# Attention and bitlinear FFN on eight cores: one clamp folded away and the transposed activations evicted by ScalarE alone

## What is computed

```python
def _act_quant(x):
    scale = 127.0 / jnp.clip(jnp.max(jnp.abs(x), axis=-1, keepdims=True), 1e-05)
    xq = jnp.clip(jnp.round(x * scale), -128.0, 127.0) / scale
    return x + jax.lax.stop_gradient(xq - x)

def _bitlinear(x, w):
    return jnp.einsum('bsi,oi->bso', _act_quant(x), _weight_quant(w))

gate = silu(_bitlinear(x, w_gate))          # 1024 -> 4096
up = _bitlinear(x, w_up)                    # 1024 -> 4096
ffn = _bitlinear(gate * up, w_down)         # 4096 -> 1024
x = _layernorm(x + ffn)
```

## Time and profile before

| | |
|---|---|
| median of 3 runs | 3895.15 us |
| profiled execution, its own time | 3897.07 us |
| span of its slowest core (core 3) | 3895.5 us |
| spans of the other cores | 3872.5 to 3888.9 us |
| core 3: TensorE busy | 1803.9 us (46%) |
| core 3: VectorE busy | 1509.8 us (39%) |
| core 3: ScalarE busy | 978.6 us (25%) |
| core 3: mean granted TensorE clock | 0.664 of full |

### The profile page before, as it was taken

One profiled execution on the slowest core, in us unless ns is written; L12 is line 12 of the kernel. 1 busy time (PEld: TensorE's weight loads), 2 busy tenths in 40 slices (PEclk: granted clock), 3 DMA queues, 4 the chain that ended last, 5 costly groups with the idle time before them and its releaser, 6 DMA issues.

```text
span 3895.5 us, 32053 instructions; the slowest of 8 cores (3872.5 to 3895.5 us)
## 1 busy us (share of the span) xinstructions
PE 1803.9 (46%) x8824; PEld 608.9 (16%) x8824; DVE 1509.8 (39%) x2965; ACT 978.6 (25%) x1164; POOL 18.7 (0%) x54
## 2 busy tenths in 40 slices
PE   1201212321034434565776775484466529552944
PEld 0000000100011111111111111232133204221421
DVE  1453474444455544322122112444244344424443
ACT  1202201220000014574875785110011001101100
POOL 1000000000000000000000000000000000000000
PEclk9998555555565555555555555697788769785967
DMA  5445343322410000101001000321242125023312
GB/s 113 162 162 173 143 181 92 81 65 78 156 35 11 0 11 6 38 1 44 1 6 38 1 1 28 124 92 38 65 145 66 50 75 163 26 61 108 111 35 71
DMA packets 140980, 278.38 MB, mean 71 GB/s; under 512 B 7944, under 2 KB 106504, under 8 KB 134664
## 3 DMA queue, kind: packets, MB, share of 16 engines
q1 hardware_dynamic: 107256, 192.96, 15.0%
q10 hardware_dynamic: 24320, 67.12, 5.1%
q0 software_dynamic: 9232, 16.25, 2.7%
HBM read 250.61 MB, written 41.94 MB: 75 GB/s over the span
## 4 chain that ended last, share of the span: by engine, by line
PE 22%; DVE 15%; ACT 14%; issue 5%; DMA 5%; DVEq 1%; ACTq 0%; SPq 0%
PE ps_f L1177 6%; PE ps_f L1063 6%; PE ps_f L1069 6%; ACT PTb L730 3%; ACT PTb L734 3%; ACT PT L730 3%; ACT PT L734 3%; DMA wdbuf<-scr_d 2%; DMA xo_t<-xo 1%; DVE den_sb L808 1%; PE ps_tf L958 1%; DVE hbuf L1127 1%; DVE hbuf L1131 1%; DVE hq L1135 1%; PE ps_sc L706 1%
## 5 line engine op out<-in xcount | busy, mean ns | idle before, releaser
L706 PE MATMUL ps_sc<-qn,khat 32*128 32x512 bf16 (+3 forms) x1280 | 313.3, 530 | 136.8 <-ACT PT L730 49.9
L1177 PE MATMUL ps_f<-wdbuf,hqT 128*128 128x512 bf16 x1024 | 300.0, 454 | 87.5 <-DMA wdbuf<-scr_d 38.5
L1063 PE MATMUL ps_f<-wgbuf,xqT 128*128 128x512 bf16 x1024 | 248.6, 387 | 113.9 <-DMA wubuf<-scr_u 113.0
L1069 PE MATMUL ps_f<-wubuf,xqT 128*128 128x512 bf16 x1024 | 245.6, 383 | 0.0
L742 DVE TENSOR_TENSOR PT<-PT,maskD 128x512 bf16<-128x512 bf16 x64 | 27.2, 425 | 489.8 <-ACT PT L734 489.8
L1083 DVE SCALAR_TENSOR_TENSOR hbuf<-ps_f,xsc,gate_s 128x512 f32<-128x512 f32 x128 | 96.1, 751 | 268.3 <-ACT gate_s L1077 268.3
L730 ACT ACTIVATE PT<-ps_sc,negMb 128x1024 bf16<-128x1024 f32 (+3 forms) x160 | 158.1, 988 | 121.0 <-PE ps_sc L706 108.7
L353 PE MATMUL ps_tr<-ident,xst 128*128 128x128 bf16 x384 | 52.2, 304 | 272.4 <-DVE xTc L29 182.0
L1077 ACT ACTIVATE gate_s<-ps_f,xsc 128x512 f32<-128x512 f32 x128 | 88.2, 689 | 345.7 <-PE ps_f L1069 345.6
L958 PE MATMUL ps_tf<-ident,hq 128*128 128x128 bf16 x512 | 59.9, 252 | 238.6 <-DVE hq L1135 238.6
L730 ACT ACTIVATE PTb<-ps_sc,negMb 128x1024 bf16<-128x1024 f32 (+3 forms) x160 | 158.1, 988 | 35.7 <-PE ps_sc L706 24.4
(11 more groups left out here) (226 smaller groups left out, 2515.7 us busy)
## 6 DMA issues: line engine op xcount, KB each, us to landing
wgbuf<-scr_g SPq DMA_DIRECT2D x32, 1024.0 KB, 6.5
wubuf<-scr_u SPq DMA_DIRECT2D x32, 1024.0 KB, 9.1
wfbuf<-wgT SPq DMA_DIRECT2D x8, 2048.0 KB, 9.8
wfbuf<-wgT ACTq DMA_DIRECT2D x8, 2048.0 KB, 8.5
wfbuf<-wuT SPq DMA_DIRECT2D x8, 2048.0 KB, 13.2
wfbuf<-wuT ACTq DMA_DIRECT2D x8, 2048.0 KB, 10.2
wfbuf<-wdT SPq DMA_DIRECT2D x32, 512.0 KB, 3.9
wfbuf<-wdT ACTq DMA_DIRECT2D x32, 512.0 KB, 4.2
```

The costliest lines, as they stand in the source:

```text
L706: e.matmul(ps_sc[:, j * 512 + stc:j * 512 + 512], khat[32 * j:32 * j + 32, gi * T + sc * 128: gi * T + sc * 128 + 128], qn[32 * j:32 * j + 32,
L1063: P.emit(t, lambda e, c=c, i4=i4, bi=bi, gb=gb: e.matmul(ps_f[:, gb:gb + 512], xqT[:, i4 * D + c * 128:i4 * D + c * 128 + 128], wgbuf[bi][ ...
L1069: P.emit(t, lambda e, c=c, i4=i4, bi=bi, ub=ub: e.matmul(ps_f[:, ub:ub + 512], xqT[:, i4 * D + c * 128:i4 * D + c * 128 + 128], wubuf[bi][ ...
L1177: e.matmul(ps_f[:, ((2 + i4) % 4) * 512: ((2 + i4) % 4) * 512 + 512], hqT[:, i4 * INNER + io * 128: i4 * INNER + io * 128 + 128], wdbuf[bi ...
```

## The change

Three edits. In `emit_xprep` and in the round of the down product, the two instructions "subtract the rounding constant and take the minimum with 127" and "take the maximum with -128 and write bf16" become one, which subtracts, takes the minimum and writes bf16; the maximum with -128 is gone. (The scale is 127 over the row's largest magnitude, so no value lies below -127.) In the round of the down product, the copies out of both PSUM banks are done by ScalarE; before, VectorE copied for row tiles 0 and 2 and ScalarE for 1 and 3. In `emit_xprep` the copies stay as they were.

```diff
-                def ftr_batch(srcs, dst_fn, extra_wait, bank):
+                def ftr_batch(srcs, dst_fn, extra_wait, bank, eng=None):
...
-                    eng, ctr = (v, cV) if bank == 0 else (s, cA)
-                    mk = P.emit(eng, lambda e, bank=bank: dst_fn(e, ps_tf[bank]),
+                    e2, ctr = (v, cV) if bank == 0 else (s, cA)
+                    if eng == "s":
+                        e2, ctr = s, cA
+                    mk = P.emit(e2, lambda e, bank=bank: dst_fn(e, ps_tf[bank]),
                                 waits=[(cT, cT.v)], incs=[(ctr, 1)])
...
-                        P.emit(v, lambda e: e.tensor_scalar(
-                            hbuf[:, 0:D], hbuf[:, 0:D], MAGIC, 127.0, ALU.subtract,
-                            ALU.min))
-                        mk_xq = P.emit(v, lambda e, i4=i4: e.tensor_scalar_max(
-                            xq[:, i4 * D:(i4 + 1) * D], hbuf[:, 0:D], -128.0),
+                        mk_xq = P.emit(v, lambda e, i4=i4: e.tensor_scalar(
+                            xq[:, i4 * D:(i4 + 1) * D], hbuf[:, 0:D],
+                            MAGIC, 127.0, ALU.subtract, ALU.min),
                             incs=[(cV, 1)])
...
-                                    P.emit(v, lambda e, hs=hs: e.tensor_scalar(
-                                        hbuf[:, hs:hs + 512], hbuf[:, hs:hs + 512],
-                                        MAGIC, 127.0, ALU.subtract, ALU.min))
                                     mk_hq = P.emit(v, lambda e, i4=i4, hs=hs:
-                                                   e.tensor_scalar_max(
+                                                   e.tensor_scalar(
                                                        hq[:, i4 * 512:i4 * 512 + 512],
-                                                       hbuf[:, hs:hs + 512], -128.0),
+                                                       hbuf[:, hs:hs + 512],
+                                                       MAGIC, 127.0,
+                                                       ALU.subtract, ALU.min),
...
-                                              [(cV, mk_hq[1])], i4 % 2)
+                                              [(cV, mk_hq[1])], i4 % 2,
+                                              eng="s")
```

## The result

The changed kernel takes 3675.61 us in the median of 8 runs (3671.77 to 3683.21), against 3895.85 us for the kernel before in the same series (8 runs, 3893.39 to 3904.88): a ratio of 0.9432, 95% interval 0.9419 to 0.9444, 220 us less. A second series gave 3674.49 us and 0.9431 (0.9418 to 0.9444). The forecast was 3691 us, in a range of 3665 to 3727.

The account below looks back on a forecast made before the run. The prediction took the time as set by engines waiting for each other, VectorE and TensorE in the down product's first half. Four chunks saving 191 us plus 12.8 from xprep made 204 us, so 3691 us, range 3665 to 3727.

Parts of the forecast that it names:

- 28 rounds: Down product's first half, seven steps in each of four chunks: a round falls from 14.26 to 8.15 us.
- first rounds: First round of each chunk, with no burst to hide in: 6.1 us in place of 11.13, saving 5.0 a chunk.
- xprep: Folded clamp in emit_xprep: 16 removed instructions of 0.80 us, all on the path, 12.8 us.
- The knot: Down-product rounds: VectorE's tile 0 copy, ahead of quantising tiles 1 to 3, waits out the burst; gap 9.27 to 3.45 us.
- The burst: A round's 16 down-product matmuls: 4.7 us, the middle between 4.0 starting at full clock and 5.36 starting at half.
- The half-clock rival: Clock stays at half through the bursts: round 10.4 us, 141 us saved, 3754; chance 0.09, shared with late weight blocks.
- The rival in which the copy's move gives nothing: Something else holds VectorE in the rounds, only removed instructions count: 81 us saved, 3814; chance 0.04.

Follow-up runs that it names:

- another order in the list: Changed kernel with all four tiles' quantisations ahead of the transposes and copies in VectorE's list, copies on both engines again: 3658.71 us, ratio 0.9391.
- the pipelined kernel: Changed kernel with the next round's transposes and copies among this round's matmuls: 3749.24 us; with the odd weight block from SyncE's queue too, 3605.5 us.

## Why the prediction was right

The forecast of 204 us less against 220 measured, term by term (mean of the cores, from the table):

| term | forecast | measured |
|---|---|---|
| 28 rounds | 171 | 184 |
| first rounds | 20 | 20.5 |
| xprep | 12.8 | 12.0 in the trace; 12.4 by the run of this edit alone (3 to 21) |
| last burst of a chunk | not counted | 3.6 |

*The knot.* That VectorE's copy, by its place in the list, held the quantisation behind the burst, and that the gap shrinks to four ScalarE copies: right. The forecast gap at the full clock was 3.32 us and the measured mean is 3.32, with the clock full in every gap. The move alone gives the short rounds, the fold alone does not, and another order in the list does as well as the move. So of the two edits in the rounds, the fold's 69 us of VectorE work bought only the first rounds' 8.6.

*The burst* is the term that was mis-sized. I took 4.7 us, the middle between 4.0 at full clock and 5.36 as before; it is 4.44. Its end at 4.0 was right (4.05 where the clock is kept, median of all 4.12), and so was its reason, the odd block's late landing: without it the median is 3.45. The mix was not the one I reasoned. I expected that the clock falls in some of the gaps, so that those bursts start at half. It falls in none: the long bursts are the first one of each chunk and the one in six that start at full and lose the clock under way. In the 28 rounds, over the cores, that is (32 x 5.7 + 32 x 5.1 + 160 x 4.05) / 224 = 4.44 us. So the two ends were right and the reason for the middle was not; that 4.7 came as near as it did is partly luck. With 0.26 us from the burst and 0.13 from the gap, for which I had taken 3.45, over 28 rounds it is 11 of the 13 us that were missing there; the rest is the 14.33 us of a round before, averaged over all cores, where I had 14.26 from one. The last bursts profit from the clock like the others, which I had left out.

*xprep.* That the removed instructions lie on the path in all four places is shown by the trace, 3.1 us in each of three and 2.9 in chunk 0, where 3.2 were forecast; the run alone would allow 3 to 21.

*The rivals.* The half-clock rival didn't come about here, but it nearly did in the fold alone, where every burst begins at half and is some 6 us, and the added matmuls showed it to be the clock. The Trainium skill, "TensorE: Matmul & The Clock Gate", section "HAM oscillation — how this bites in real kernels", has a loop whose waits are long enough to drop the clock, so that every burst pays the ramp again. The traces of the kernel before and of the fold alone agree, with gaps of 9.1 and 7.6 us and 256 of 256 bursts that begin at half. By the same traces the changed kernel isn't such a loop: with gaps of 3.3 us, none of the 224 bursts behind a chunk's first begins at half. The rival in which the copy's move gives nothing was priced at 81 us for the fold alone, and that price was wrong: 40 us, since three tiles and not four lie in a gap, and the clock took back 0.82 us a round. ScalarE's copies stay at 588 ns or less, now 128 of them on each core.

## What to carry to other kernels

Look in a two-way wait for the instruction whose place in an in-order list holds work that could run earlier; moving it to an idle engine or behind that work are the same cure as long as the bursts cover what the first engine has left to do, and shortening the instructions around it is a poor one (19 of the 184 us). Where nothing waits for the copies any more, the engine does matter: 42 us in the pipelined kernel. When work has left the path, ask next what the queue that received it also holds: here a weight load stood behind the copies and cost half a microsecond a round, and in the pipelined kernel four. And count a shorter gap between bursts of matmuls twice, as time and as clock, with its sign open until measured: the fold alone shortened the gap by 1.5 us and lengthened the burst by 0.8, the other order in the list shortened both.

## What was not expected of the hardware

The granted clock can take back half of a gain: in the fold alone a round with 1.5 us less of gap had bursts 0.8 us longer, all of them alike (5.7 to 6.2 us in nine of ten, where the kernel before has 4.6 to 6.4), at a mean clock of 0.64. Why the clock comes back later in those bursts than in the kernel before is not shown. Twelve added matmuls a gap brought it to 0.98 and made the kernel 70 us faster by doing more. In the changed kernel's gaps of 3.3 us stand 16 transposes, and the clock stays full through all of them; where it falls, in 36 of 224 bursts, it does so in the first 0.9 us of the next burst. With gaps of 2.8 us (the other order in the list) it falls in one of 224, and with four matmuls of 128x512 in each gap in none.
